# Attention of layer 0: gates, queries and keys by group, output products among the value products, and the values' bias once per bank

## The reference

```python
# query: (L=16 batches, B=128 tokens, E=128); EH = 256
q = query.transpose(1, 0, 2); shortcut = q            # (128 tokens, 16, 128)
xn = layernorm(q) * ln_g + ln_b
u    = silu(xn @ Wu.T + bu)                           # gates, 256 wide
v    = silu(xn @ Wv.T + bv)                           # values, 256 wide
base = silu(xn @ Wb.T + bb)                           # 128 wide
quad_q, quad_k = rope(base * qqw + qqb), rope(base * qkw + qkb)
kernel = square(relu(quad_q @ quad_k.T / 64 + bias))  # causal
out = (u * (kernel @ v)) @ Wo.T + bo + shortcut
```

## Time and profile before

| | before |
|---|---|
| median of three runs | 544.58 us (543.71 to 545.65) |
| profiled execution, its own time | 544.83 us |
| its span, first to last instruction | 543.0 us |
| mean granted TensorE clock | 0.932 of full |
| busy: PE / PEld / DVE | 452.4 / 305.5 / 432.0 us |
| busy: ACT / POOL | 241.5 / 52.9 us |

### The profile page before, as it was taken

The page is one execution under the profiler, slowest core; times in us unless marked ns, Lnnn a source line. Parts: engine busy times, 40 slices in busy tenths (PEclk is TensorE's granted clock), DMA queues, the critical chain, the costliest instruction groups (busy, mean ns, idle before and its releaser), DMA issues.

```text
span 543.0 us, 8998 instructions
## 1 busy us (share of the span) xinstructions
PE 452.4 (83%) x3484; PEld 305.5 (56%) x3484; DVE 432.0 (80%) x883; ACT 241.5 (44%) x406; POOL 52.9 (10%) x69
## 2 busy tenths in 40 slices
PE   3999978999799867600399989999999999999763
PEld 1448978997259552200169975566656556555410
DVE  6889999885776559998844467956798999997887
ACT  5668735562561065895444573335223323421300
POOL 2050000000190029600000000000000000000000
PEclk9999989999899897955599996999999999999999
DMA  6992966900050005500620000039930000000000
GB/s 218 418 370 61 336 229 249 321 33 0 13 144 2 0 2 154 193 0 0 245 114 1 2 1 0 2 117 369 369 94 2 10 6 7 6 6 11 5 12 13
DMA packets 20352, 56.13 MB, mean 103 GB/s; under 512 B 2595, under 2 KB 5030, under 8 KB 20310
## 3 DMA queue, kind: packets, MB, share of 16 engines
q1 hardware_dynamic: 19872, 55.46, 28.9%
q10 hardware_dynamic: 438, 0.11, 0.1%
HBM read 53.36 MB, written 1.15 MB: 100 GB/s over the span
## 4 chain that ended last, share of the span: by engine, by line
PE 63%; DVE 29%; issue 5%; ACT 2%; DMA 0%; DVEq 0%
PE bk L662 15%; PE bk L670 8%; DVE XT L1479 7%; PE bk L366 5%; DVE QS L1247 5%; PE bk L707 5%; PE bk L388 4%; PE bk L361 3%; PE bk L603 2%; DVE RC L1000 2%; PE bk L557 2%; PE bk L499 2%; DVE RA L1240 1%; PE bk L472 1%; PE bk L481 1%
## 5 line engine op out<-in xcount | busy, mean ns | idle before, releaser
L1479 DVE SCALAR_TENSOR_TENSOR XT<-bk,WK,XT 128x128 f32<-128x128 f32 x256 | 89.0, 349 | 8.8 <-PE bk L707 0.4
L662 PE MATMUL bk<-X,RB 128*128 128x512 f16 x384 | 95.3, 385 | 0.0
L917 ACT ACTIVATE X<-RA 128x512 f16<-128x512 f32 x64 | 40.1, 630 | 105.0 <-DVE RA L1494 80.4
L707 PE MATMUL bk<-RB,RA 128*128 128x512 f16 x192 | 52.8, 389 | 11.4 <-DVE XT L1479 8.7
L662 PEld LDWEIGHTS bk<-X,RB 128*128 128x128 f16 x384 | 36.8, 99 | 44.6 <-issue 5.0
L670 PEld LDWEIGHTS bk<-RB,X 128*128 128x128 f16 x768 | 48.9, 99 | 15.4 <-issue 0.6
L670 PE MATMUL bk<-RB,X 128*128 128x128 f16 x768 | 54.0, 220 | 0.0
L366 PE MATMUL bk<-X,RC 128*128 128x128 f16 x768 | 48.7, 221 | 1.9 <-DVE RC L1000 1.7
L366 PEld LDWEIGHTS bk<-X,RC 128*128 128x128 f16 x768 | 46.1, 99 | 3.8 <-issue 3.0
L1467 DVE TENSOR_TENSOR X<-RA,X 128x512 f16<-128x512 f32 x64 | 43.8, 684 | 2.1 <-ACT X L917 2.1
L773 ACT ACTIVATE WK<-bk 128x512 f32<-128x512 f32 x48 | 28.6, 596 | 29.9 <-PE bk L366 20.4
(11 more groups left out here) (287 smaller groups left out, 768.7 us busy)
## 6 DMA issues: line engine op xcount, KB each, us to landing
RA<-in_wx SPq DMA_DIRECT2D x27, 768.0 KB, 5.8
RC<-expert_weights SPq DMA_DIRECT2D x22, 256.0 KB, 5.9
STG<-in_w SPq DMA_DIRECT2D x8, 512.0 KB, 3.5
RC<-in_wx SPq DMA_DIRECT2D x5, 768.0 KB, 5.6
RC<-in_w SPq DMA_DIRECT2D x8, 384.0 KB, 4.7
STG<-in_w SPq DMA_DIRECT2D x6, 384.0 KB, 7.2
WBOT<-expert_weights SPq DMA_DIRECT2D x8, 256.0 KB, 6.5
STG<-expert_weights SPq DMA_DIRECT2D x6, 256.0 KB, 8.7
```

Source lines behind the costliest of these rows:

```text
L662: t = e.matmul(BK[m][:, :], P16[:, wp, wo:wo + 128], ZH[:, n % 4, xp, :], start=(e1 == 0 and i == 0), stop=(e1 == 15 and i == 2))
L707: t = e.matmul(bank_o(n)[:, :], OT16[:, xp, bb_(4 * c + b)], P16[:, wp, 6144 + 512 * g:6656 + 512 * g], start=(i == 0), stop=(i == 2))
L917: e.activation(ZH[:, r, 0, :], zf[r], ACT.Copy).then_inc(S("z_hi"), 1)
L1479: stt(XT[:, bb_(t_)], bank_o(n)[:, bb_(i)], RW[:, t_, e1:e1 + 1], XT[:, bb_(t_)], ALU.mult, ALU.add).then_inc(S("acc"), 1)
```

## The change

- `QQ` and `QK` are laid out by group: the 32 steps of L1555 and of L1223 read 128 columns in token order and write them 128 elements apart (512 bytes), eight short columns per group. L481 then reads blocks that lie side by side.
- The gates `u0` and `u1` are laid out by group as well: eight of the twelve silus of L806 write with the same step (`base` stays in token order). The gating L1240 then works on columns that lie side by side, and so does L499, which now makes the output of four groups and no longer of four batches.
- `x1` (L1244) therefore reads and writes `XT` with a step of 16 elements, for four groups. The LoRA products, which go by batch, wait for all four `x1`.
- TensorE's order becomes kernel products 0 to 3, value products 0 and 1, output 0, value 2, output 1, value 3, output 2, output 3; output c waits for the eight gatings no more but for the first 2c + 2. VectorE's becomes gatings 0 to 2, x1(0), gating 3, x1(1) to x1(3).
- The values' bias is one pass of 512 columns per bank, first in the bank, and not one of 256 per group, last.
- `womm` and `x1` move to other lanes.

```diff
@@ views
-        qqv = QQ.rearrange("p (m t) -> p t m", t=16)
-        qkv = QK.rearrange("p (m t) -> p t m", t=16)
+        def grouped(ap, m0, m1):
+            return ap.rearrange("p (t m) -> p m t", t=16)[:, m0:m1, :]
+        def by_token(ap):
+            return ap.rearrange("p (m t) -> p m t", t=16)
@@ values, TensorE
+                both = BK[bk][:, :].rearrange("p (t f) -> p t f", t=2)
+                e.matmul(both, ON3[:, :], BV3[:, 3, :].unsqueeze(1).to_broadcast([3, 2, 256]), start=True, stop=False, skip_group_check=True)
                 for h in range(2):
-                    o = BK[bk][:, 256 * h:256 * h + 256]
                     for n, (wp, xp) in enumerate(SPLIT):
-                        e.matmul(o, xnv[xp][:, 2 * t2 + h, :], AW16[:, wp, 256:512], start=(n == 0), stop=False)
-                    t = e.matmul(o, ON3[:, :], BV3[:, 3, :], start=False, stop=True)
+                        t = e.matmul(both[:, h, :], xnv[xp][:, 2 * t2 + h, :], AW16[:, wp, 256:512], start=False, stop=(h == 1 and n == 2), skip_group_check=True)
@@ kernel, value and output products, TensorE
-                    t = e.matmul(BK[c % 2][:, bb_(i)], qkv[:, 4 * c + i, :], qqv[:, 4 * c + i, :], start=True, stop=True)
+                    t = e.matmul(BK[c % 2][:, bb_(i)], QK[:, bb_(4 * c + i)], QQ[:, bb_(4 * c + i)], start=True, stop=True)
...
-            for c in range(4):
-                q.wait_ge("g", 8)
+            def output_product(c):
+                q.wait_ge("g", 2 * c + 2)
                 q.wait_ge(*(("u1", 3 + c) if c < 2 else ("x1", c - 1)))
...
+            for c in range(4):
+                kernel_product(c)
+            value_product(0)
+            value_product(1)
+            output_product(0)
+            value_product(2)
+            output_product(1)
+            value_product(3)
+            output_product(2)
+            output_product(3)
             for c in range(4):
-                q.wait_ge("x1", c + 1)
+                q.wait_ge("x1", 4)
@@ silus, ScalarE
-                    e.activation(dst[:, cc(c)], BK[4 + c][:, :], ACT.Silu, bias=col(b), scale=1.0 / AS).then_inc(S(name), 1)
+                    to, of = (dst[:, cc(c)], BK[4 + c][:, :]) if name == "base" else (grouped(dst, 32 * c, 32 * c + 32), by_token(BK[4 + c][:, :]))
+                    e.activation(to, of, ACT.Silu, bias=col(b), scale=1.0 / AS).then_inc(S(name), 1)
@@ sine part, VectorE
-                        stt(dst[:, bb_(l)], BSW[:, bb_(l)], ROPE[:, o + 1, l:l + 1], dst[:, bb_(l)], ALU.mult, ALU.add).then_inc(S("sin"), 1)
+                        to = grouped(dst, 8 * l, 8 * l + 8)
+                        stt(to, by_token(BSW[:, bb_(l)]), ROPE[:, o + 1, l:l + 1], to, ALU.mult, ALU.add).then_inc(S("sin"), 1)
@@ gating and x1, VectorE
-                    uv = U[ch].rearrange("p (m t) -> p t m", t=16)[:, 4 * c:4 * c + 4, :]
-                    tt(uv, uv, BK[2 + 2 * (c % 2) + ch][:, :].rearrange("p (t m) -> p t m", t=4), ALU.mult).then_inc(S("g"), 1)
+                    uv = U[ch][:, cc(c)]
+                    tt(uv, uv, BK[2 + 2 * (c % 2) + ch][:, :], ALU.mult).then_inc(S("g"), 1)
...
-                q.wait_ge("xq", c + 1)
-                stt(XT[:, cc(c)], BK[6 + c % 2][:, :], col("bo"), XT[:, cc(c)], ALU.add, ALU.add).then_inc(S("x1"), 1)
+                q.wait_ge("xq", 4)
+                to = XT[:, :].rearrange("p (m t) -> p t m", t=16)[:, 4 * c:4 * c + 4, :]
+                stt(to, four(BK[6 + c % 2][:, :]), col("bo"), to, ALU.add, ALU.add).then_inc(S("x1"), 1)
+            for c in range(3):
+                gated_values(c)
+            x1(0)
+            gated_values(3)
+            for c in range(1, 4):
+                x1(c)
@@ cosine part, GpSimd
-                        e.tensor_scalar(dst[:, bb_(l)], BASE[:, bb_(l)], ROPE[:, o, l:l + 1], ROPE[:, o + 2, l:l + 1], ALU.mult, ALU.add).then_inc(S("cos"), 1)
+                        e.tensor_scalar(grouped(dst, 8 * l, 8 * l + 8), by_token(BASE[:, bb_(l)]), ROPE[:, o, l:l + 1], ROPE[:, o + 2, l:l + 1], ALU.mult, ALU.add).then_inc(S("cos"), 1)
```

More of the change, by code:

```diff
@@ L47 @@
 LANES = [
-    (("up", 48), ("basemm", 4), ("u0mm", 4), ("u1mm", 4), ("vmm", 8), ("kmm", 4), ("gmm", 8), ("womm", 4), ("loramm", 4),
+    (("up", 48), ("basemm", 4), ("u0mm", 4), ("u1mm", 4), ("vmm", 8), ("kmm", 4), ("gmm", 8), ("loramm", 4),
      ("ffmm", 24), ("ffdown", 12), ("x3mm", 4), ("mlp_up", 16), ("prod_q", 60)),
@@ L52 @@
     (("mean", 4), ("rstd", 4), ("vvmm", 4), ("turn0", 1), ("qkvmm", 12)),
-    (("varmm", 4), ("ppmm", 4), ("logits", 4), ("turnw", 3), ("scores", 4)),
+    (("varmm", 4), ("womm", 4), ("ppmm", 4), ("logits", 4), ("turnw", 3), ("scores", 4)),
     (("x4mm", 4), ("spread", 16), ("xtmm", 4)),
@@ L61 @@
     (("x_hi", 4), ("wt16", 1), ("wts", 3), ("ot_hi", 4)),
-    (("gated", 48), ("weff", 4), ("diag", 4), ("fw_lo", 3), ("sin", 32), ("k", 4), ("g", 8), ("x1", 4), ("l_max", 4), ("l_lo", 4),
+    (("gated", 48), ("weff", 4), ("diag", 4), ("fw_lo", 3), ("sin", 32), ("k", 4), ("g", 8), ("l_max", 4), ("l_lo", 4),
      ("ff_max", 24), ("gate16", 4), ("gated_ff", 4), ("ot_ff", 4), ("o_lo", 12), ("x2", 4), ("pp", 4), ("w2", 2), ("weighed", 64)),
-    (("h_lo", 16), ("xg", 4), ("kadd", 4), ("l_hi", 4), ("g2_max", 4), ("gated16_0", 1), ("o_max", 4), ("o_hi", 12), ("x4", 4), ("zlo", 64)),
+    (("h_lo", 16), ("xg", 4), ("kadd", 4), ("x1", 4), ("l_hi", 4), ("g2_max", 4), ("gated16_0", 1), ("o_max", 4), ("o_hi", 12), ("x4", 4), ("zlo", 64)),
     (("q", 4), ("norm0", 1), ("xn", 4), ("sn", 1), ("part_max", 5), ("rs", 4)),
@@ L468, in tensor, with kernel_product @@
                 q.wait_ge(*(("fw_lo", bk + 1) if t2 < 3 else ("xg", 4) if t2 == 3 else ("v", t2 - 3)))
+                both = BK[bk][:, :].rearrange("p (t f) -> p t f", t=2)
+                e.matmul(both, ON3[:, :], BV3[:, 3, :].unsqueeze(1).to_broadcast([3, 2, 256]), start=True, stop=False, skip_group_check=True)
                 for h in range(2):
-                    o = BK[bk][:, 256 * h:256 * h + 256]
                     for n, (wp, xp) in enumerate(SPLIT):
-                        e.matmul(o, xnv[xp][:, 2 * t2 + h, :], AW16[:, wp, 256:512], start=(n == 0), stop=False)
-                    t = e.matmul(o, ON3[:, :], BV3[:, 3, :], start=False, stop=True)
+                        t = e.matmul(both[:, h, :], xnv[xp][:, 2 * t2 + h, :], AW16[:, wp, 256:512], start=False, stop=(h == 1 and n == 2), skip_group_check=True)
                 t.then_inc(S("vmm"), 1)
-            for c in range(4):
+            def kernel_product(c):
                 q.wait_ge("sin", 32)
@@ L480, in tensor, with value_product @@
                 for i in range(4):
-                    t = e.matmul(BK[c % 2][:, bb_(i)], qkv[:, 4 * c + i, :], qqv[:, 4 * c + i, :], start=True, stop=True)
+                    t = e.matmul(BK[c % 2][:, bb_(i)], QK[:, bb_(4 * c + i)], QQ[:, bb_(4 * c + i)], start=True, stop=True)
                 t.then_inc(S("kmm"), 1)
-            for c in range(4):
+            def value_product(c):
                 for ch in range(2):
@@ L1234, in vector, with gated_values @@
                 stt(kt, kt, 0.0, kt, ALU.max, ALU.mult).then_inc(S("k"), 1)
-            for c in range(4):
+            def gated_values(c):
                 for ch in range(2):
@@ L1238, in vector, with x1 @@
                     q.wait_ge("u1", 4)
-                    uv = U[ch].rearrange("p (m t) -> p t m", t=16)[:, 4 * c:4 * c + 4, :]
-                    tt(uv, uv, BK[2 + 2 * (c % 2) + ch][:, :].rearrange("p (t m) -> p t m", t=4), ALU.mult).then_inc(S("g"), 1)
-            for c in range(4):
+                    uv = U[ch][:, cc(c)]
+                    tt(uv, uv, BK[2 + 2 * (c % 2) + ch][:, :], ALU.mult).then_inc(S("g"), 1)
+            def x1(c):
                 q.wait_ge("womm", c + 1)
-                q.wait_ge("xq", c + 1)
-                stt(XT[:, cc(c)], BK[6 + c % 2][:, :], col("bo"), XT[:, cc(c)], ALU.add, ALU.add).then_inc(S("x1"), 1)
+                q.wait_ge("xq", 4)
[7 more added lines that the diff above has]
+                x1(c)
             def absmax(dst, src):
```

## The result

The changed kernel takes 545.70 us in the median of 20 runs (544.73 to 547.32); the kernel before, in 20 runs beside them, 543.63 (541.62 to 545.65). The ratio is 1.0036, 95% interval 1.0025 to 1.0048: 2.1 us slower, where 541.4 us and a gain of 3.3 were forecast. A second measurement on another chip gave 1.0037 (1.0015 to 1.0059).

What follows compares the result with a forecast made beforehand. Bound by a chain of engine work (63% TensorE, 29% VectorE, almost no DMA). Saving 4.43 us from kernel to LoRA products, less 1.1 us for later rotary steps, gives -3.3 and 541.4 us; range 538.8 to 543.9.

Steps and rivals of the forecast that it cites:

- landmark 1: First cosine step to first kernel product, 18.1 us before; forecast 1.1 us longer (bounds -0.8 and +2.7).
- landmark 2: First kernel product to first LoRA product, 25.22 us before in the forecast; 20.79 claimed, 4.43 us saved.
- Part 4: Rotary steps with scattered output: GpSimd 0.045 us more per step, contention 0.4 us; kernel products start 1.1 us later.
- Rival (c): GpSimd's scattered rotary step sets the kernel products' start outright: 0.2 us more per step, +6.0, 546.4 us; chance 0.08.
- The clock beyond the stretch: Behind the rewritten stretch, a shift changes where TensorE's clock falls: about 1 us uncertainty either way.
- rival (b): Scattered rotary writes double per element, GpSimd pays 0.09 us: +2.7, some 1 more by clock; 543.0 to 544.0; chance 0.16.
- The wait of 0.46 us ahead of output 0: TensorE waits 0.46 us for VectorE's first two gatings before output product 0.
- The clock fall ahead of the output products: Slow output-product passes after 2.02 us of idle TensorE cost 1.9 us, over two fifths of the 4.43 saved.
- Part 3: Values' bias once per bank: 0.8 us saved (0 to 1.7), wholly beside the rotary steps, so worth nothing.
- Part 5: Eight gate silus with 512-byte step: bounds 0.69 and 1.06 us, 1.02 start to start; projections wait 0.2 us, hidden.

Runs made afterwards that it cites:

- run 4: Changed kernel with VectorE's sine steps held until GpSimd had made all 32 cosine steps (one execution): 549.95 us.
- run 1: Changed kernel with queries and keys back in token order, gates by group, new product order and single bias pass kept: 541.05 us, ratio 0.9951.
- run 2: Kernel before with only queries and keys laid out by group: 546.56 us, ratio 1.0053.
- the runs under 5: Changed kernel with unread passes keeping TensorE busy ahead of the first feed-forward products: 42 passes 543.52 us (1.0009), 31 passes 543.78 us (0.9999).
- run 7: Changed kernel with 22 unread passes on TensorE between the last value pass and the first kernel product: 543.48 us, ratio 1.0017.
- run 3: Changed kernel with the loops of the cosine and sine steps swapped (target in runs of 8, source read 64 bytes apart): 544.76 us, ratio 1.0016.

## Why the prediction was wrong

The forecast was 3.3 us less than before, measured were 2.1 more. The 5.4 us between them are 2.8 at landmark 1 (3.89 lost for 1.1), 0.5 at landmark 2 (3.94 gained for 4.43) and 1.7 to 2.8 in the feed-forward part, by the two profiled executions.

**Part 4, the contention between the rotary steps: here it failed.** The sum was 0.4 us for contention, 1.4 for GpSimd's write and 0.4 for VectorE's last five steps, landmark 1 at 166.85 - 147.53 = 19.3 with a far bound of 20.9. It is 22.02. GpSimd's own write was over-priced (0.02 us per step for 0.045, 0.7 us in all for 1.4), VectorE's about right (0.10 for 0.09), and contention under-priced some nine times: GpSimd's 32 steps took 4.2 us more, of which the write by itself is 0.7, so 3.5 for my 0.4. The five sine steps behind GpSimd's end took 1.6 us for 1.3. I had scaled the slowdown of before (26%) by VectorE's added busy time. But the slowdown is itself a function of how both access memory: GpSimd's distance from start to start beside VectorE grew from 0.529 to 0.703 us with a sine step only 0.10 us longer. Run 4 shows it by taking the overlap away and nothing else, runs 1 and 2 that it is in the layout of queries and keys. Rival (c) had the path right, GpSimd's steps and nothing else set when the kernel products start, but gave the cost to the write itself. By its own sum the gain was used up at 0.67 us per step over all 32; they took 0.637, and that already used up 3.89 of the 3.94 us that there were.

**The clock beyond the stretch: the second miss.** I gave it 1 us either way as noise. It is a term: the feed-forward part took 2.77 and 1.72 us more in the two profiled executions, and the runs under 5 show 1.7 to 2.2 us of the medians in it. Inside the stretch, run 7 shows 2.0 us of the median in the wait of 5.5 us ahead of the kernel products; only rival (b) had a fall of the clock there, at 1 us, and the sum had none. Why the clock rises later in the feed-forward part after the change is open: the input comes at the same distances in both (the table's +0.10). It is not one part of the change alone, since the same stretch is 2.1 us longer than before in run 1 and 1.4 in run 2. For the kernel before it rests on one profiled execution.

**What held.** Landmark 2: 20.79 forecast, 21.19 measured, 20.1 with the clock held. L1261, the gating by group, is at 684 ns in the median (680 forecast), `x1` at 1079 (1120), and TensorE's waits ahead of the last output product (0.23 us for 0.43) and ahead of the LoRA products (1.16 for 1.3) are there. The wait of 0.46 us ahead of output 0 is not, because the kernel and value products ended late. The clock fall ahead of the output products is gone; there is one ahead of the kernel products in its place.

**Mis-sized, and hidden.** Part 3: a bank takes 1.13 us (155.26 to 156.39), not 1.28, so 2.0 us less for the values and not 0.8. The bias pass costs the 0.32 that I gave it; the six value passes take 0.81 and not 0.96. Run 1 shows 1.0 of the 2.0 as time. I had called the saving worth nothing, which is true only of the changed kernel. Part 5: the eight scattered silus take 1.14 to 1.30 us each, above my bound of 1.06, but 0.90 from start to start, below the 1.02 that I counted with; TensorE waited 0.34 + 0.57 us for their banks and not 0.2, still beside the rotary steps.

Of the Trainium skill's two rules, that of "GPSIMD Engine Reference" ("Performance pitfalls for Q7 kernels"), which charges GpSimd for reads with a step and says nothing of writes, agrees with both runs: in run 4 the scattered write alone costs 0.02 us per step, in run 3 the read with a step alone costs 0.10. "Advanced Engine Details and Errata" ("SBUF Cachelines") agrees with the silus (0.65 to 0.90 us from start to start) and with VectorE's steps (0.27 to 0.36), but not with GpSimd's write. What decided, the pace of the two engines side by side, is in neither of the sentences that I drew on.

## What to carry to other kernels

When two engines work through the same data side by side, price a new access pattern by the pace of both together; the pace alone, of either, says little (0.46 us for GpSimd and 0.36 for VectorE here, and GpSimd at 0.70 beside VectorE). A layout change moves cost to whoever writes the layout: look whether that writer has slack before counting the reader's gain. A stretch whose pace is set by another engine hides a half clock of TensorE, but only until its input is all there; here it was still low at that moment after the change and not before it.

## What the runs showed that was not expected

- GpSimd's step of 128 elements, at 0.43 to 0.46 us from start to start alone in both layouts, took up to 1.73 us beside VectorE's two-input step when both wrote with a 512-byte step (0.60 at most before).
- Swapping the loops, so that the target has runs of 32 bytes and the source the step of 64, gave back 1 us of 4 at landmark 1: less contention (0.73 us at most beside VectorE), but 0.53 us per step alone.
- ScalarE's silu of 512 elements from PSUM: 688 ns with a target side by side, 1137 to 1295 with the 512-byte step; 0.65 and 0.90 us from start to start.
- Idle-time passes of TensorE are worth 1.7 to 2.0 us where its clock would be low when its work arrives, showed no gain where another engine sets the pace, and held back work where they stood ahead of it: eight of them took 3.1 us in place of 2.3, and 13 stood on the chain for 3.6.
